# Conditioned attention block on one core: the first of eight rounds written in another order, and one copy moved in every later round

## What is computed

```python
def block(x, t, gamma_a, beta_a, alpha_a, W_q, W_k, W_v, W_o,
          gamma_f, beta_f, alpha_f, gate_w, hidden_w, out_w, out_b):
    # gamma_a .. alpha_f are (t @ w.T)[:, None, :], one row for each sequence
    rms = lambda z: z * rsqrt(mean(z * z, -1) + 1e-6)
    h = gamma_a * rms(x) + beta_a
    q, k, v = split16(h @ W_q.T), split16(h @ W_k.T), split16(h @ W_v.T)
    x = x + alpha_a * (softmax(0.25 * q @ k.T) @ v) @ W_o.T
    h = gamma_f * rms(x) + beta_f
    return x + alpha_f * (silu(h @ gate_w.T) * (h @ hidden_w.T) @ out_w.T + out_b)

def final(x, t, weight, bias, lin_w, lin_b):
    out = layernorm(x) * weight + bias + tanh(t @ lin_w.T + lin_b)[:, None, :]
    return out * weight + bias
```

## Time and profile before

| what | value |
|---|---|
| median of 3 runs | 530.4 us (530.06 to 531.44) |
| profiled execution, its own time | 530.51 us |
| its span in the trace | 528.6 us |
| PE busy | 483.1 us (91% of the span), 4446 matmuls |
| weight loads of PE busy | 403.3 us (76%) |
| DVE busy | 392.3 us (74%) |
| POOL busy | 277.9 us (53%) |
| ACT busy | 239.5 us (45%) |
| chain that ended last | PE 80%, DVE 7%, ACT 4%, DMA 3%, POOL 3% |
| mean granted clock of PE | 0.969 |

### The profile page before, as it was taken

The page is one execution under the profiler, slowest core; times in us unless marked ns, Lnnn a source line. Parts: engine busy times, 40 slices in busy tenths (PEclk is TensorE's granted clock), DMA queues, the critical chain, the costliest instruction groups (busy, mean ns, idle before and its releaser), DMA issues.

```text
span 528.6 us, 11662 instructions
## 1 busy us (share of the span) xinstructions
PE 483.1 (91%) x4446; PEld 403.3 (76%) x4446; DVE 392.3 (74%) x772; ACT 239.5 (45%) x347; POOL 277.9 (53%) x182
## 2 busy tenths in 40 slices
PE   7768739999999999999999999999999999999990
PEld 4555627788788897889787987889787988798880
DVE  5846635887878688877888787967888788875636
ACT  3454624333836264443725274534635374513240
POOL 3335455646336843585446841594456834517471
PEclk9979968999999999999999999999999999999996
DMA  8483152220540317030640327030721234220121
GB/s 218 145 202 74 59 140 66 61 62 1 145 136 22 81 28 230 21 93 6 161 117 20 79 73 204 2 97 0 202 75 35 64 91 108 62 61 0 41 57 63
DMA packets 36234, 45.00 MB, mean 85 GB/s; under 512 B 3312, under 2 KB 30704, under 8 KB 36208
## 3 DMA queue, kind: packets, MB, share of 16 engines
q1 hardware_dynamic: 36208, 44.64, 31.9%
HBM read 35.97 MB, written 4.47 MB: 76 GB/s over the span
## 4 chain that ended last, share of the span: by engine, by line
PE 80%; DVE 7%; ACT 4%; DMA 3%; POOL 3%; issue 1%; SPq 1%; ACTq 0%; DVEq 0%; POOLq 0%
PE banks L650 32%; PE banks L667 17%; PE banks L466 7%; PE banks L568 6%; PE banks L600 4%; PE banks L502 4%; PE banks L586 3%; PE banks L591 3%; ACT qpair L843 2%; DVE x2n L1065 2%; PE banks L573 1%; PE banks L621 1%; DMA work_c<-x2n 1%; DMA xtok<-x_in 1%; PE banks L531 1%
## 5 line engine op out<-in xcount | busy, mean ns | idle before, releaser
L650 PE MATMUL banks<-x2s,gh 128*128 128x512 f32 x768 | 193.3, 401 | 8.9 <-ACT x2s L898 8.4
L650 PEld LDWEIGHTS banks<-x2s,gh 128*128 128x128 f32 x768 | 141.3, 190 | 41.6 <-issue 9.0
L1426 POOL TENSOR_TENSOR hs<-act_t,hs 128x512 fp32r<-128x512 f32 x64 | 83.1, 1302 | 99.9 <-ACT hs L879 99.9
L667 PE MATMUL banks<-wout,hs 128*128 128x256 f32 x768 | 104.5, 286 | 1.3 <-POOL hs L1426 1.3
L667 PEld LDWEIGHTS banks<-wout,hs 128*128 128x128 f32 x768 | 97.7, 188 | 6.6 <-POOL hs L1426 1.7
L879 ACT ACTIVATE hs<-act_t 128x512 fp32r<-128x512 f32 x64 | 40.3, 630 | 90.5 <-DVE act_t L1200 84.5
L1196 DVE SCALAR_TENSOR_TENSOR act_t<-act_t,banks 128x512 f32<-128x512 f32 x64 | 43.9, 686 | 49.5 <-ACT act_t L872 49.2
L872 ACT ACTIVATE act_t<-banks 128x512 f32<-128x512 f32 x64 | 38.3, 598 | 84.4 <-PE banks L650 81.6
L1147 DVE RECIPROCAL work_c<-banks 128x512 f32<-128x512 f32 x16 | 53.7, 3354 | 10.3 <-PE banks L586 10.3
L1200 DVE SCALAR_TENSOR_TENSOR act_t<-act_t,banks 128x512 f32<-128x512 f32 x64 | 44.0, 687 | 5.4 <-PE banks L650 1.2
L466 PE MATMUL banks<-xs,wqk 128*128 128x512 f32 x192 | 46.8, 393 | 0.7 <-ACT xs L813 0.7
(11 more groups left out here) (120 smaller groups left out, 699.2 us busy)
## 6 DMA issues: line engine op xcount, KB each, us to landing
xtok<-x_in SPq DMA_DIRECT2D x8, 512.0 KB, 5.4
xres<-x_in SPq DMA_DIRECT2D x8, 512.0 KB, 7.1
row_aa<-rows_dram SPq DMA_DIRECT2D x16, 256.0 KB, 6.8
row_af<-rows_dram SPq DMA_DIRECT2D x16, 256.0 KB, 5.5
row_b<-rows_dram SPq DMA_DIRECT2D x16, 256.0 KB, 6.1
shift<-rows_dram SPq DMA_DIRECT2D x16, 256.0 KB, 6.1
work_c<-xn SPq DMA_DIRECT2D x14, 256.0 KB, 3.8
y<-final SPq DMA_DIRECT2D x7, 512.0 KB, 3.2
```

The lines of the kernel that those rows point to most:

```text
L650: last = mm(banks[:, base + part, :], gh[:, a, k, w:w + P], x2s[:, b, k, :], start=(n == 0), stop=(n == 5))
L667: last = mm(banks[:, t // 2, D * (t % 2):D * (t % 2) + D], hs[:, c % 2, b, P * t:P * t + P], wout[:, a, c, :], start=(c == 0 and a == b an ...
L1426: tt(hs[:, c % 2, 1, :], act_t[:, c % 2, :], hs[:, c % 2, 0, :].bitcast(F32), ALU.subtract)\
```

## The change

The work of group 1 in `first()` is arranged anew, and one thing changes in all rounds.

- Group 1's normed x is made as group 0's is. Its transposed load, the store and load of 1/rms and the three POOL steps are gone. POOL scales the tokens (new, 128x1024), PE transposes them behind `attend(0, 1)`, DVE does gamma and beta (four operations of 512 columns) behind `normalise(0, 1)`. The second x is loaded in the layout of the first one (runs of 1 KB instead of 4 KB).
- The selectors are built on ACT, ahead of the k copies; the tanh of the shift vector follows it. `finish_shift` stands on POOL right behind the scaling of the tokens.
- `move_v(0)` stands on SP ahead of stages 5 and 6 instead of behind them, with `xn` as its source, and waits for v alone; `move_v(1)` waits for v alone.
- Stage pieces 2 to 7 are cut at other places on ACT and POOL.
- On PE the output projection of group 0 stands ahead of k and v of group 1, with 16 fill matmuls ahead of it (instead of none there); 4 instead of 10 ahead of the transposes of x2n, and none instead of 8 behind them; q of group 1 stands behind the transposes. `head(1)` is now used for group 1 too.
- In every `head`, ACT makes all four q copies; tanh of chunk 0 is the first instruction of `main`.

The diff, without hunks that only rename a function's argument or repeat the above for the last group (the `v_kept` buffer becomes `xn` for all groups, semaphore counts of `xn_gamma`, `xn_scaled` and `ld_xt` drop by one):

```diff
@@ -53,7 +53,7 @@
 SETUP_TANH, SETUP_ALPHAS, SETUP_SHIFT = 1, 4, 3
 
 
-WARM_LOADS, WARM_MAX, WARM_OUTPUT, WARM_NORM, WARM_SPLIT = 3, 4, 4, 10, 8
+WARM_LOADS, WARM_MAX, WARM_OUTPUT, WARM_NORM = 3, 4, 16, 4
 LAST_DVE = 3
 ZEROED = 1
 RSQRT_MAGIC = float(0x5F3759DF)
...
@@ -278,11 +278,13 @@
 
             def load_x(g):
 
-                if not later(g):
+                if not rowed(g):
+                    if g:
+                        sp.wait_ge(xt_mm, 1)
                     sp.dma_start(xtok[:, :, :], x_v[g]).then_inc(ld_x, 16)
                     return
-                if isinstance(g, int) and g == 1:
-                    sp.wait_ge(xt_mm, 1)
+                if isinstance(g, int):
+                    sp.wait_ge(xt_mm, 2)
                 sp.wait_ge(x_stats, XS * g)
                 sp.dma_start(xtok[:, :, :], x_run[g]).then_inc(ld_x, 16)
 
...
@@ -331,10 +333,8 @@
             def move_v(g):
 
                 sp.wait_ge(v_out, g + 1)
-                if not later(g):
-                    sp.wait_ge(xn_gamma, 1)
                 for e in range(2):
-                    sp.dma_start(v_swapped[64 * e:64 * e + 64], v_kept(g)[64 - 64 * e:128 - 64 * e])\
+                    sp.dma_start(v_swapped[64 * e:64 * e + 64], v_kept[64 - 64 * e:128 - 64 * e])\
                         .then_inc(v_moved, 16)
 
             def store(f):
@@ -348,18 +348,15 @@
             sp.dma_start(linw, linT).then_inc(ld_linw, 16)
             load_stage(0)
             load_stage(1)
-            sp.dma_start(work_c[:, :, :], xT_v[1]).then_inc(ld_xt, 16)
             for dst, src in ((lnw_b, lnw), (lnb_b, lnb), (linb_b, linb), (outb_b, outb_dram)):
                 sp.dma_start(dst, src.to_broadcast([P, D])).then_inc(ld_lin, 16)
             load_x(1)
             load_stage(2)
             load_stage(3)
-            store_rs(1)
             load_stage(4)
-            load_rs(1)
+            move_v(0)
             load_stage(5)
             load_stage(6)
-            move_v(0)
             sp.wait_ge(setup_dve, SETUP_ALPHAS)
             sp.dma_start(rows_dram[:, 0:R_SHIFT, :], rows[:, 0:R_SHIFT, :]).then_inc(rows_stored, 16)
             load_res(0)
...
@@ -442,11 +438,14 @@
                 mm(banks[0:B, 2, 0:D], cond, linw, start=True, stop=True)
                 mm(banks[0:B, 2, D:2 * D], cond, tabw[:, AA, :], start=True, stop=True).then_inc(rows_mm, 1)
 
-            def transpose_x():
-                pe.wait_ge(xs_scaled, 1)
+            def transpose_x(g):
+
+                pe.wait_ge(xs_scaled, 2 * g + 1)
+                if later(g):
+                    pe.wait_ge(p_ready, 3)
                 steps = [(t, k) for t in range(TT) for k in range(KD)]
                 for n, (t, k) in enumerate(steps):
-                    if n == len(steps) // 2:
+                    if not later(g) and n == len(steps) // 2:
                         pe.wait_ge(xs_scaled, 2)
                     last = nc.tensor.transpose(banks[:, 4 + k, P * t:P * t + P],
                                                xtok[:, t, P * k:P * k + P], ident)
...
@@ -516,13 +511,13 @@
                 elif n == 0:
                     pe.wait_ge(v_out, g + 1)
                     pe.wait_ge(q_ready, 4 * g + 2)
+                elif n == 1:
+                    pe.wait_ge(q_ready, 4 * g + 4)
+                    pe.wait_ge(qpair_ready, 4 * g + 4)
                 else:
                     pe.wait_ge(max_ready, 4 * g + n - 1)
                 if n == 0:
                     pe.wait_ge(k_ready, 4 * g + 2)
-                if n == 1 and later(g):
-                    pe.wait_ge(q_ready, 4 * g + 4)
-                    pe.wait_ge(qpair_ready, 4 * g + 4)
                 h, base = n // 2, bank_of_s(g, n)
                 for i in range(4):
                     b = 4 * (n % 2) + i
@@ -669,12 +664,15 @@
                                   stop=(c == CH - 1 and b == 1 and t % 2 == 1))
                 last.then_inc(out_mm, 1)
 
-            def head(g):
+            def head(g, ln=True):
 
                 k_proj(g)
                 v_proj(g)
+                if not ln:
+                    warm_up(wqk[:, 0, 0], WARM_NORM, 0)
                 transpose_x2(g - 1)
-                ffn_out(g - 2, CH - 1)
+                if ln:
+                    ffn_out(g - 2, CH - 1)
                 q_proj(g)
 
             def first():
@@ -697,13 +695,9 @@
                 attend(0, 0)
                 scores(0, 3)
                 attend(0, 1)
-                k_proj(1)
-                v_proj(1)
+                transpose_x(1)
+                warm_up(wqk[:, 0, 0], WARM_OUTPUT, 2)
                 o_proj(0)
-                q_proj(1)
-                warm_up(wqk[:, 0, 0], WARM_NORM, 0)
-                transpose_x2(0)
-                warm_up(wqk[:, 0, 0], WARM_SPLIT, 0)
 
             def main(g):
 
...
@@ -914,50 +909,43 @@
                 keep_v(g)
                 place_v_kept(g)
                 x2_split(g - 1)
-                pair_q(g, (1,))
-                tanh(g - 1, 0)
-                pair_q(g, (0,))
+                pair_q(g)
 
             def first():
                 cut_hi(0)
                 cut_hi(1)
                 setup_identity()
                 x0_split()
+                nc.scalar.activation(sel[:, :, :].rearrange("p c (e k) -> p (c e) k", e=2),
+                                     cst[:, C_SEL:C_SEL + 2 * G * SEQ].unsqueeze(2).to_broadcast([P, 2 * G * SEQ, L]),
+                                     ACT.Copy).then_inc(selectors_ready, 1)
+                act.wait_ge(setup_dve, SETUP_TANH)
+                nc.scalar.activation(cvec, cvec, ACT.Tanh).then_inc(setup_act, 1)
                 pair_k(0, range(2))
                 pair_q(0)
                 par_k()
                 keep_v(0)
                 act.wait_ge(zeroed, ZEROED)
                 place_v_kept(0)
-                act.wait_ge(setup_dve, SETUP_TANH)
-                nc.scalar.activation(cvec, cvec, ACT.Tanh).then_inc(setup_act, 1)
+                cut_hi(2)
+                cut_hi(3)
                 place_v_swapped(0)
                 exp(0, 0)
                 exp(0, 1)
-                xs_split(1)
-                cut_hi(2)
+                cut_hi(4)
                 exp(0, 2)
                 exp(0, 3)
-                cut_hi(3)
+                cut_hi(5)
                 o_split(0, 0)
-                cut_hi(4)
-                pair_k(1, (0,))
+                cut_hi(6)
                 o_split(0, 1)
-                pair_k(1, (1,))
-                par_k()
-                keep_v(1)
-                place_v_kept(1)
-                cut_hi(5)
-                pair_q(1)
-                cut_hi(6)
-                x2_split(0)
                 cut_hi(7)
-                tanh(0, 0)
+                xs_split(1)
 
             def main(g, ln=True):
                 f = g - 1
 
-                hidden_hi(f, 0)
+                feed(f, 0)
                 place_v_swapped(g)
                 for c in range(1, 4):
                     feed(f, c)
...
@@ -1246,6 +1235,8 @@
                 setup_weights()
                 normalise(0, 0)
                 normalise(0, 1)
+                for k in range(KD):
+                    scale_shift_xn(1, k, x0_steps, 4 + 2 * k).then_inc(xn_beta if k else x0_steps, 1)
                 residual1(0)
                 stats_x2(0)
                 norm2(0)
...
@@ -1436,22 +1423,18 @@
                 cut_lo(0)
                 pool.wait_ge(xs_lo, 1)
                 cut_lo(1)
-                pool.wait_ge(ld_tables, LD_TABLE)
-                nc.gpsimd.tensor_copy(sel[:, :, :].rearrange("p c (e k) -> p (c e) k", e=2),
-                                      cst[:, C_SEL:C_SEL + 2 * G * SEQ].unsqueeze(2).to_broadcast([P, 2 * G * SEQ, L]))\
-                    .then_inc(selectors_ready, 1)
-                gamma_xn(1)
-                scale_xn(1)
-                shift_xn(1)
-                xs_split(1)
+                pool.wait_ge(norm1_steps, RS * 2)
+                tt(xtok[:, :, :], xtok[:, :, :], nt1[:, 1, 0, :].unsqueeze(2).to_broadcast([P, TT, D]),
+                   ALU.mult).then_inc(xs_scaled, 1)
+                finish_shift()
                 cut_lo(2)
-                o_split(0, 0)
                 cut_lo(3)
-                o_split(0, 1)
                 cut_lo(4)
                 cut_lo(5)
+                o_split(0, 0)
+                o_split(0, 1)
                 cut_lo(6)
-                finish_shift()
+                xs_split(1)
 
             def main(g, ln=True):
                 f = g - 1
```

45 lines of the change are left out of this document (19 added, 26 removed).

## The result

The changed kernel takes **508.31 us** (median of 4 runs, 506.9 to 508.42); the kernel before took 530.8 beside it (4 runs, 530.06 to 531.44). The ratio is **0.9571**, with a 95% interval of 0.9549 to 0.9593. The profiled execution took 508.42 with a span of 506.6 (before: 530.51 and 528.6). Both spans are compared from here on.

What follows compares the result with a forecast made beforehand. It took PE as the bound, 91% busy, with only its waits worth anything, mostly in the first round. 19.0 there plus 3.0 in the loop made 22.0 off 530.5: 508.5, with an 8-in-10 range of 504.5 to 513.

Steps and rivals of the forecast that it cites:

- Squares: DVE at the second x: two squares lose 2.5 of blocking by POOL, and 0.66 of load wait goes too.
- the bound "nothing": Second x's load: none of the 0.66 wait is won if 1 KB runs land later than 4 KB runs.
- ACT ahead of the k copies: Selectors and tanh of the shift, 2.0 plus 0.4, fit ACT's idle 2.90 with 0.5 to spare: cost 0.
- The move: Moved v lands in the usual 3.8, placing at 29.8, not 35.83; exp and third scores come 6.0 earlier.
- `attend(0, 1)`: PE in the first round: its end comes at 42.8 instead of 48.84.
- third scores come 6.0 earlier and all after it with them: PE's third scores, at 38.21 before, shift 6.0 earlier, and the end of attend(0, 1) with them.
- bound (20.2 in place of 19.0): Gain up to tanh of chunk 0 if PE keeps its full clock at the third scores.
- The slower rival: PE stays at its lower clock from 42.8 to tanh: 532.4; chance 0.03, a part of it another 0.03.
- PE from 42.8 on: Transposes and fills to 47.8, then output projection, k, v, fills; x2n at 57.5 instead of 66.4, q to 61.4.
- A square meets POOL: Rival: POOL's low piece of x1 runs late and holds a square of x2, up to 2.2 more, 510.7; chance 0.08.
- The gate: From x2n's transposes to tanh: beta, high piece and q copies put tanh of chunk 0 at 64.6, not 83.55.
- The loop: Later rounds: PE's wait passes from q copies to chunk 0's product, winning 0.5 a round, 3.0 over six.

Runs made afterwards that it cites:

- e2: Kernel before, with POOL waiting for the second x's Newton steps before building the selectors: 528.57 us, ratio 0.9955.
- e4: Changed kernel, with the move of v behind the loads of stages 5 and 6 again: 507.82 us, ratio 0.9569.
- e10: Kernel before, with loads of stages 4 to 6 issued ahead of the store and load of 1/rms: 527.33 us median of ten.
- e11: Kernel before, with q copies ahead of tanh, POOL waiting for Newton steps, loads ahead of 1/rms, weight pieces and shift steps early: 511.32 us, ratio 0.9623.
- e1: Kernel before, with all four q copies on ACT ahead of tanh of chunk 0 in every head: 528.66 us, ratio 0.9965.
- e3: Kernel before, with ACT cutting stage 6 ahead of group 1's q copies instead of behind them: 526.5 us, ratio 0.9923.
- e9: Kernel before, with the shift's POOL steps and the cuts of stages 5 and 6 made early, x1 as before: 521.06 us, ratio 0.9809.
- e5: Changed kernel without the 16 fill matmuls ahead of the output projection: 508.33 us, ratio 0.9562.
- e12: Changed kernel, POOL's low piece of x1 ahead of stage 6's, and k's matmuls on high pieces of x1 first: 508.34 us, ratio 0.9566.

## Why the prediction was right, point by point

- **Squares.** The 2.5 of blocking went (e2 alone: 2.48). The 0.66 for the second x did not: with 512 KB less ahead of it in the queue it still came at 16.77 against 16.70. The term missed that SP issues this load only behind PE's transposes of the first x, at 10.18 before and 10.44 now. This is the bound "nothing", not the one taken, and the chain up to v ran 0.7 behind the forecast for it.
- **ACT ahead of the k copies.** Cost 0, as said; 0.76 of idle time was left where 0.5 was expected.
- **The move.** The landing held (3.6 for its two halves, 3.8 forecast), and so did the size. The reason was half wrong: the text gave weight to stages 5 and 6 standing behind the move. e4 puts them ahead of it and loses nothing. What counts is that no load is held back by 1/rms any more: with the old source and place of the move, the placing comes 4.3 behind v's copy in e10 and e11, and 7.3 before.
- **`attend(0, 1)`.** Forecast 42.8, measured 40.5. The third scores started at 32.89, 0.7 behind the forecast 32.2. But from there to the end of `attend(0, 1)` 7.59 passed, where 10.63 did before; the step "third scores come 6.0 earlier and all after it with them" kept the old length. Of the 3.0, 1.6 are PE's clock, which did not fall: the third scores took 1.16, not 1.66, and the sums behind them 1.07, not 1.93. The other 1.4 are a stop of PE in the kernel before, inside the last 64 matmuls of the values, for which the profile names no releaser:

```profile
48.37 0.53 PE L591 MATMUL banks<-pt,vblk 128*32 128x64 f32 x21 [1.13 <-issue]
```

It stands between the same two matmuls in e1 (2.49), e3 (1.95) and e9 (1.08), and not in e2, e10, e11 or the changed kernel. In e1 the third scores took 1.16 too and PE was 1.3 earlier at these matmuls, and still it went on behind the stop at 48.39, against 48.37 before. So there the stop set the end, not the clock. In all four a transfer of the DMA queue for instructions starts some 2.4 us before PE goes on; whether PE waited for it was not tested. No term of the prediction held this. Its bound (20.2 in place of 19.0) covered the clock alone, so that 20.1 was measured is in part luck.
- **The slower rival.** PE at its lower clock needed PE's hole near 31 to be felt behind 43. The clock from 45 to 50 was 1.00. With the fills taken out it does fall, to 0.77 (e5), and even then the time stays.
- **PE from 42.8 on.** 16 fills took 3.91 (3.9 forecast). The step "k to 53.6, v to 56.5" took PE as never waiting. k waited 1.58 for POOL, so x2n (55.4) was complete before PE was through with v and its fills (near 56.6): part of the 2.1 won earlier was given back here.
- **A square meets POOL.** It happened on a small scale: 0.45, at 50.15, of the rival's up to 2.2. The squares came 2.4 earlier than thought (52.6), the low piece only 0.6 (it ended at 50.75, forecast 51.4), so the two met.
- **The gate.** Beta to high piece and q copies ran as put: from the end of q (60.3 here, 61.4 forecast) to tanh 3.1 us, forecast 3.2. The wait for the high piece is 0.43.
- **The loop.** The mechanism was right: the wait changes hands. Its size was off: 1.9 for six rounds, 3.0 forecast. From the start of the q projection to the gate of chunk 1 a round takes 6.92 (175.63 to 182.55) and took 7.59 before (195.25 to 202.84), so 0.67 is won there, a little over the 0.6. The term "slack of 0.8 against a shift of 0.6 + 0.2" was too kind: the output product at 197.52 takes 1.82 where it took 1.70. Another 0.2 goes between the next two output products (6.50 from start to start, 6.30 before), which the prediction did not look at. Over a whole round 58.38 became 57.99, and 0.4 is left of 0.67.

The total, 508.3 against 508.5, is close partly because a gain taken too small (1.1 in the first round) and one taken too large (1.1 in the loop) cancel.

## What to carry to other kernels

Take one instant on which all later work hangs, and follow each engine's order up to it: here almost all of the 22 us lay ahead of one tanh, held by weight pieces and shift steps that stood, in program order, in front of work that others waited for. When a piece of work is moved out of the chain, look at what stands on the other engines at its new place; e3 lost 3 of its 8 us to POOL pieces of 2.5 beside two squares, and in e12 a piece of 2.4 held beta for 0.6. Before a reordering is credited to one of its moves, undo that move alone: the place of the move of v and the 16 fills cost or bring nothing, and the place of the output projection is worth 12, though only with the new way of making x1: e11 has the old place with the old way and is 3.1 behind.
